# Moving two shared groups of the last stage behind its ten sorted groups

## What is computed

```python
probs = softmax(gelu(xf @ router_w1 + router_b1) @ router_w2 + router_b2)
topk_p, topk_i = top_k(probs, 2)              # 2 of 8 experts per token
v, integrated = zeros_like(xf), xf
for _ in range(2):
    ctx = concatenate([integrated, v])
    x_sh, v_sh = inl(shared(ctx), integrated, v)
    x_r,  v_r  = weighted sum over the token's 2 experts of inl(expert(ctx), integrated, v)
    x_next, v_next = sw * x_sh + (1 - sw) * x_r, sw * v_sh + (1 - sw) * v_r
    halt = sigmoid(gelu(integrated @ halt_w1 + halt_b1) @ halt_w2 + halt_b2)
    integrated += halt * (x_next - integrated); v += halt * (v_next - v)
out = xf + integration_weight * (gelu(integrated @ refine_w1 + refine_b1) @ refine_w2 + refine_b2)
```

## Time and profile before

| what | value |
|---|---|
| runs | 995.5, 994.6, 991.86 us; median 994.6 |
| profiled execution | 991.68 us |
| its span on the core | 989.9 us |
| mean granted PE clock | 0.922 |
| PE busy | 782.1 us, 79% |
| DVE, ACT, POOL busy | 58%, 57%, 49% |
| wait of the SP token loads for the last write-back | one, 59.5 us |

### The profile page before, as it was taken

How to read it: one execution, slowest core, us unless ns; L and a number is a source line. 1 busy time by engine, 2 the same in 40 slices (tenths; PEclk the granted TensorE clock), 3 DMA queues, 4 the chain that set the end, 5 groups by cost and what they waited for, 6 DMA issues and landing times.

```text
span 989.9 us, 13034 instructions
## 1 busy us (share of the span) xinstructions
PE 782.1 (79%) x3904; PEld 535.8 (54%) x3904; DVE 577.9 (58%) x1438; ACT 566.4 (57%) x1003; POOL 488.1 (49%) x436
## 2 busy tenths in 40 slices
PE   7799997587888877999999856575576668877477
PEld 4588886444444435767676644454344444544255
DVE  6622333648888682222434588658566877586655
ACT  5744444544445304635544539877666898788532
POOL 1411202335554486224434777537777775467750
PEclk9999999799999997999999969887898999888789
DMA  9940000000000000000000535657557664633124
GB/s 344 423 136 1 0 1 1 1 1 0 1 1 1 0 1 0 1 1 1 1 1 27 186 92 152 207 158 226 166 175 238 202 191 146 196 121 101 48 78 128
DMA packets 75921, 92.90 MB, mean 94 GB/s; under 512 B 24032, under 2 KB 61920, under 8 KB 73808
## 3 DMA queue, kind: packets, MB, share of 16 engines
q1 hardware_dynamic: 65248, 65.87, 20.7%
q0 software_dynamic: 10464, 25.66, 8.1%
q10 hardware_dynamic: 144, 0.59, 0.2%
HBM read 45.95 MB, written 46.13 MB: 93 GB/s over the span
## 4 chain that ended last, share of the span: by engine, by line
PE 46%; DVE 16%; POOL 11%; ACT 11%; issue 9%; DMA 5%; POOLq 0%; DVEq 0%; SPq 0%; ACTq 0%
PE PS L1945 7%; PE PS L1954 6%; POOL tokens L693 4%; POOL KEEP L770 3%; PE PS L1752 3%; PE PS L1723 3%; PE PS L1864 3%; PE PS L1960 3%; PE PS L1832 3%; POOL slots L684 3%; PE PS L1713 2%; DMA KEEP<-moved,small 2%; DVE TEMP L961 2%; PE PS L1660 2%; PE PS L2058 2%
## 5 line engine op out<-in xcount | busy, mean ns | idle before, releaser
L2069 PE MATMUL PS<-TEMP,KEEP 128*128 x320 | 116.9, 508 | 36.9 <-ACT TEMP L1569 30.4
L770 POOL DMA_INDIRECT KEEP<-moved,small x96 | 104.4, 1087 | 69.9 <-issue 35.4
L675 POOL DMA_INDIRECT slots<-KEEP,small x96 | 101.1, 1053 | 47.2 <-issue 27.4
L2069 PEld LDWEIGHTS PS<-TEMP,KEEP 128*128 128x128 f32 x320 | 66.5, 223 | 65.1 <-issue 50.7
L1509 ACT ACTIVATE KEEP<-PS,TEMP 128x512 f32<-128x512 f32 x96 | 63.5, 690 | 58.0 <-PE PS L1945 57.1
L1569 ACT ACTIVATE TEMP<-PS 128x512 f32<-128x512 f32 (+2 forms) x92 | 51.5, 561 | 78.3 <-DVE TEMP L1180 77.7
L621 POOL TENSOR_TENSOR KEEP<-KEEP 128x1024 f32<-128x1024 f32 x32 | 63.7, 2005 | 53.6 <-PE PS L1864 51.8
L1945 PE MATMUL PS<-TEMP_R 128*128 128x512 f32 x288 | 77.1, 422 | 4.2 <-POOL TEMP_R L715 3.8
L2091 PE MATMUL PS<-KEEP,TEMP 128*64 128x128 f32 x480 | 40.2, 308 | 42.2 <-issue 19.1
L1864 PE MATMUL PS<-KEEP,TEMP 128*128 128x512 f32 x128 | 62.7, 619 | 9.3 <-DVE TEMP L961 8.2
L1945 PEld LDWEIGHTS PS<-TEMP_R 128*128 128x128 f32 x288 | 56.2, 198 | 20.1 <-POOL TEMP_R L715 4.2
(11 more groups left out here) (275 smaller groups left out, 1877.5 us busy)
## 6 DMA issues: line engine op xcount, KB each, us to landing
slots<-LX SPq DMA_DIRECT2D x14, 1024.0 KB, 25.8
moved<-LX SPq DMA_DIRECT2D x20, 512.0 KB, 3.3
TEMP<-slots SPq DMA_DIRECT2D x20, 512.0 KB, 3.8
TEMP<-experts SPq DMA_DIRECT2D x80, 64.5 KB
TEMP<-seconds SPq DMA_DIRECT2D x1, 3072.0 KB
TEMP<-early SPq DMA_DIRECT2D x1, 2765.0 KB, 12.0
TEMP<-experts SPq DMA_DIRECT2D x80, 32.5 KB
TEMP<-slots SPq DMA_DIRECT2D x10, 258.0 KB, 3.8
```

The source lines that it names most:

```text
L675: pool.indirect_dma_start(dst, bass.IndirectOffsetOnAxis(ap=pos[:, h, 2 * m + k:2 * m + k + 1], axis=0), src, None).then_inc(SC[h], 16)
L770: pool.indirect_dma_start(G[:, n % 4, k, 0:w], None, src, bass.IndirectOffsetOnAxis(ap=pos[:, h, 2 * m + k:2 * m + k + 1], axis=0))\
L2069: last = pe.matmul(o, hT[:, e % 3, P * j:P * (j + 1)], EW2[:, 384 * (j % 2):][:, bass.ds(at[j], n)], start=True, stop=True)
```

## The change

The last stage's shared groups are split: shared groups 0 and 1 stay ahead of the ten sorted groups, 2 and 3 come behind them. So g42 and g43 are shared, g44 to g53 sorted, g54 and g55 shared. The third entry of `LATE_STARTS` follows from 46 to 44. The three first slots' loads of that stage are put in SP's list three steps ahead of the first sorted group instead of four (so at step 41, where it was 42); the entry for 32 keeps four and that for 16 keeps three. `UPDATES` is not changed.

```diff
-          ("S", 0, 2, 0, 4), ("E", 0, 2, 0, 10), ("S", 1, 2, 0, 4), ("E", 1, 2, 0, 10))
+          ("S", 0, 2, 0, 4), ("E", 0, 2, 0, 10), ("S", 1, 2, 0, 2), ("E", 1, 2, 0, 10), ("S", 1, 2, 2, 4))

-LATE_STARTS = (16, 32, 46)
+LATE_STARTS = (16, 32, 44)

                 for f in LATE_STARTS:
-                    if s == (f - 3 if f == LATE_STARTS[0] else f - 4):
+                    if s == (f - 4 if f == LATE_STARTS[1] else f - 3):
                         for g in (f, f + 1, f + 2):
                             load_in(g)
```

## The result

The changed kernel takes 999.65 us (median of 7 runs) against 995.1 us for the kernel before in 7 runs of the same comparison; ratio 1.0067, 95% interval 1.0043 to 1.0091, so 6.7 us slower (0.0067 x 995.1), with 4.3 to 9.1 in the interval. The two medians by themselves lie 4.6 us apart, inside the same interval. The profiled execution has a span of 1002.0 us.

A forecast was written before the change was run, and what follows sets the result against it. No engine fills the span; the end's chain runs through GpSimd's issues. Sequence 4's turn moves from 963.17 to 974.6, +11.4 us: 1003.1 on the profiled run, 1006.0 on the median; forecast 1004, range 995.5 to 1011.

The forecast's parts named there:

- Joint 1: TensorE's turn of g44 waits for half 1's scatter: turn at 843.5, 7.4 us hole, result at 878.2, only 6.0 sooner.
- rival C: Pipeline from g44's turn fills as slowly as before (38.5 us): +15.2, 1006.9; forecast with C (over +5) 0.74.
- The queue: SP's loads delay the store before GpSimd's first gather by 7 us, to near 858; hidden, some 10 us of cover.
- Joint 2: GpSimd writes g44 and g45 back ahead of gathers 5 to 8: 16 issues, last gather 15.8 us later, at 940.3.
- The tail: At the end, 15 write-backs after the last gather are hidden; sequence 4's turn starts at 974.6, +11.4 us.
- behind it the same 26.7 us follow: After sequence 4's turn on TensorE, the remaining work was to take an unchanged 26.7 us.
- Rival A: Groups' pace alone decides: +6.3 with GpSimd at 1.26 per issue, +3.1 if never binding; low end with D 0.20.
- Rival B: Tail's wait falls away, faster: sum -1.8, at best -4.4; needs g44's result before 867; with other overlooked gains 0.06.
- Rival D: Order doesn't act, GpSimd's queue decides either way: within 3 us of 991.7; with A's low end 0.20.

The follow-up runs named there:

- the stores first: Changed kernel with SP's stores of g40 and g41 put ahead of the weight and slots' loads of steps 42 and 43: ratio 1.0077 to the kernel before.
- both of GpSimd's edits: Changed kernel with half 0's second-iteration gathers and updates at steps 44 to 52, and each step's gathers ahead of its write-backs: ratio 1.0025 to the kernel before.
- without the hole: Changed kernel with the slots' loads of g44 to g46 taking half 0's long-written slots, so computing with other rows: ratio 1.0012 to the kernel before.
- one shared group behind and GpSimd's edits: Kernel before with only shared group 3 behind the sorted groups, updates at 44 to 52, a step's gathers ahead of its write-backs: ratio 0.9981.
- the gathers ahead: Changed kernel with each step's gathers put ahead of its write-backs on GpSimd, update steps unchanged: ratio 1.0061 to the kernel before.

## Why the prediction was right, and where its size was off

The forecast was slower, 1004 us with a range from 995.5 to 1011; measured 999.65. By its own steps, against the traces (all from g39, so that the 5.1 us ahead of the change don't enter):

- *Joint 1.* g44's turn forecast at 843.5, that is +15.9: +15.5. Its result forecast at 878.2, +50.6: VectorE's L1235 ends at 881.87 + 0.69, +49.8. Half 0's joint was a good ruler, slow transposes included. g43's control matmuls were to start 7.4 us late and start 7.1 late (+17.3 for +10.1). From the turn to the result it is 34.3 us, beside the 34.7 of the forecast and the 38.5 of *rival C*, which falls with it. Taking most of the wait away gave 5.5 us of 6.7.
- *The queue.* The first gather was forecast near 858, +30.4, and hidden: +31.1, and the stores first changed nothing behind them.
- *Joint 2.* 16 issues to g46's first write-back in 21.9 us: 904.85 - 882.84 = 22.0. The last gather 15.8 us later: 14.5, the missing 1.3 us being 0.8 from g44's result and the rest the issues' rate. That no pause would follow the first write-back held.
- *The tail.* The last write-back and its tokens were to be hidden: no wait in brackets. Sequence 4's turn was to start behind sequence 3: it does. +11.4 forecast, +9.2 found: the 1.3 of the last gather and 0.9 from there to the turn (33.4 us for 34.3).
- **The failing term** is "behind it the same 26.7 us follow". It was 24.6 (1002.0 - 977.4). The 26.7 held two pieces at the slow clock: four transposes, 1.08 in the earlier trace rows and 0.60 now, and four L2160, 3.58 and 1.98; together 2.1 us. I had the wait of 4.4 us in the sum, but not what it did to the clock of the work behind it, though I had named just that at the other joint. With 2.1 and the 2.2 of the turn off, 11.4 becomes 7.1; the traces have 7.0.
- *Rival A*, the groups' pace, was refuted in its strong form (order worth nothing) by both of GpSimd's edits together, 6.3 us in the traces. Its form with GpSimd at 1.26 us an issue gave +6.3, nearer to the measured 6.7 than my 11.4, but by luck: the issues took 1.36 and the last gather came 14.5 us later, not 10.7. Its low end had lain at +3.1; what the changed kernel has without the hole, +2.1 by the trace, isn't that rival, since the last gather is 8.4 us late there. *Rival B* fell with g44's result at +49.8 instead of the +39.4 that it needed (867). *Rival D* fell with the last gather at +111.3.
- The 1004 was also lifted by 0.9 because before's profiled execution lay under its median. Against the medians of the comparison the forecast shift of 11.4 would have been 1006.5; so the low base hid 2.5 us of the miss, which is in the shift, 11.4 for 6.7.

What stays open: why traces with the same instructions differ by up to 8 us ahead of g39. In the pair above all of the 5.1 us had arisen by 568 us; none of the runs was made to find the cause.

## What to carry to other kernels

An order that hides one queue's tail behind other work must be followed through every list that carries a fixed place in it: here the updates' steps stayed at 45 to 53 while ten groups moved up two places, so the write-backs overtook the gathers on which the groups wait. Before work is moved in front of a joint, look at how late the joint's input is: two shared groups had been covering the path from scatter over load to first turn, and taking them away opened a hole of 10 us to close a wait of 4.4. And when a single edit does nothing, look in its trace whether its own bound moved: two edits of 0.4 and 1.0 us gave 6.3 together.

## What was not expected of the hardware

The wait at sequence 4's turn costs more than its length: with it, the granted clock over the following 18 us was 0.81 and eight instructions took 2.1 us more, without it 1.00. All fourteen traces divide this way. In the five with a wait ahead of this turn (6.32, 4.41, 3.29, 2.18 and 1.48 us) the four L2160 behind it took 3.53 to 3.78 us, in the nine without one 1.98. With the two short waits the four transposes still ran at full speed (0.63), and the slow clock came only after them; with one shared group behind and GpSimd's edits (2.18 us) PE's timeline has:

```profile
963.36 0.63 PE L1666 MATMUL PS<-WL,KEEP 128*128 128x128 f32 x4 [2.18 <-DVE KEEP L1276]
964.77 3.53 PE L2160 MATMUL PS<-KEEP,WL 128*128 128x512 f32 x4 [0.78 <-ACT KEEP L1637]
```

So even the wait of 1.48 us, in the kernel with the gathers ahead, was followed by slow matmuls: the windows of that trace have 1.00 granted from 970 to 972 and 0.50 from 972 to 974. It cost 1.7 us more than its length.

GpSimd's indirect issues, 0.94 to 0.98 us each in over half of the lines, kept their mean in the changed kernel, gap included: 1.36 from the first write-back to the last gather ((944.06 - 882.84) / 45), against 1.375 before.
